# Shared-expert phase of a macaron network: logits two units behind a tile's turn, choice and places one unit later

## The reference, cut to what matters

```
h_s = _experts_mlp(u, g_shared, W1_s, b1_s, W2_s, b2_s).sum(axis=-2)
scores = jax.nn.sigmoid(u @ centroids)
gpk, i_topk = jax.lax.top_k(scores, K)            # K = 2 of 8
gk = gpk / scores.sum(axis=-1, keepdims=True)
routed_all = _experts_mlp(u, g_routed, W1_r, b1_r, W2_r, b2_r)
routed_topk = jnp.take_along_axis(routed_all, i_topk[..., None], axis=2)
h_r = (gk[..., None] * routed_topk).sum(axis=-2)
return u + h_s + h_r
```

## Time and profile before

| What | Value |
|---|---|
| median of 3 runs | 2846.81 us (2840.81 to 2848.97) |
| the profiled execution | 2843.61 us, span 2841.7 us |
| busy: PE, DVE, ACT, POOL | 82%, 70%, 50%, 44% of the span |
| ffn1a, shared-expert phase | about 1230 to 1494 us of the span |
| ffn1b, shared-expert phase | about 2216 to 2478 us of the span |
| granted TensorE clock, mean over the span | 0.904 of full |

### The profile page before, as it was taken

How to read it: one execution, slowest core, us unless ns; L and a number is a source line. 1 busy time by engine, 2 the same in 40 slices (tenths; PEclk the granted TensorE clock), 3 DMA queues, 4 the chain that set the end, 5 groups by cost and what they waited for, 6 DMA issues and landing times. The chain is left out here.

```text
span 2841.7 us, 51583 instructions
## 1 busy us (share of the span) xinstructions
PE 2337.6 (82%) x14828; PEld 1665.2 (59%) x14828; DVE 1996.4 (70%) x5346; ACT 1414.1 (50%) x2782; POOL 1258.1 (44%) x1094
## 2 busy tenths in 40 slices
PE   6559898999999896778898899388888788898890
PEld 5435454454444454756776677266667676677670
DVE  7666666666676665778786677388887787776675
ACT  4204454455454444656665566333332767566560
POOL 3242311221131122628773555476665287745551
PEclk9759999999999997888999999699999888999995
DMA  2031122121122213411135566110000111356556
GB/s 65 15 42 28 26 35 36 25 34 32 31 29 32 36 24 83 156 49 37 43 111 171 202 218 218 52 30 22 22 15 0 37 41 41 126 180 214 201 197 178
DMA packets 140628, 222.67 MB, mean 78 GB/s; under 512 B 21327, under 2 KB 100993, under 8 KB 129884
## 3 DMA queue, kind: packets, MB, share of 16 engines
q1 hardware_dynamic: 122203, 185.46, 23.8%
q0 software_dynamic: 18176, 34.14, 3.5%
HBM read 136.75 MB, written 57.32 MB: 68 GB/s over the span
## 5 line engine op out<-in xcount | busy, mean ns | idle before, releaser
L951 DVE TENSOR_REDUCE attn_rowmax<-psum 128x1 f32<-128x512 f32 (+3 forms) x748 | 457.3, 637 | 290.5 <-PE psum L789 289.8
L733 ACT ACTIVATE attn_probs<-psum 128x512 f32<-128x512 f32 (+1 forms) x704 | 387.0, 560 | 486.5 <-PE psum L852 478.7
L787 PE MATMUL psum<-attn_ks,attn_qs 72*128 72x512 bf16 (+3 forms) x1088 | 311.2, 321 | 39.4 <-DVE attn_rowmax L951 32.4
L850 PE MATMUL psum<-attn_qs,attn_ks 75*128 75x512 bf16 (+3 forms) x1024 | 288.0, 313 | 36.7 <-issue 26.2
L1287 POOL DMA_INDIRECT experts_answers<-ffn1b_y_rows,ffn1b_out_row x156 | 155.9, 999 | 151.9 <-ACT ffn1b_y_rows L1357 111.9
L789 PE MATMUL psum<-attn_mask_qk,attn_ident_b 128*128 128x128 bf16 x1088 | 222.0, 229 | 0.0
L1287 POOL DMA_INDIRECT experts_answers<-ffn1a_y_rows,ffn1a_out_row x156 | 156.9, 1006 | 146.8 <-ACT ffn1a_y_rows L1357 108.9
L850 PEld LDWEIGHTS psum<-attn_qs,attn_ks 75*128 75x128 bf16 x1024 | 101.0, 100 | 190.1 <-ACT attn_probs L733 99.5
L649 POOL TENSOR_TENSOR attn_rstd<-attn_var_eps,minus_half 128x4 f32<-128x4 f32 x18 | 18.3, 1019 | 436.4 <-DVE attn_var_eps L928 436.4
L852 PE MATMUL psum<-attn_mask_kq,attn_ident_b 128*128 128x128 bf16 x1024 | 204.0, 225 | 0.0
L867 PE MATMUL psum<-attn_probs,attn_v_aug 128*32 128x512 f32 (+3 forms) x2048 | 196.7, 462 | 0.0
(11 more groups left out here) (424 smaller groups left out, 6430.9 us busy)
## 6 DMA issues: line engine op xcount, KB each, us to landing
ffn1a_w_ring<-experts_packed SPq DMA_DIRECT2D x39, 1026.5 KB, 5.1
ffn1b_w_ring<-experts_packed SPq DMA_DIRECT2D x39, 1026.5 KB, 5.2
attn_qs<-attn_qparts SPq DMA_DIRECT2D x216, 64.0 KB
attn_ks<-attn_kparts SPq DMA_DIRECT2D x216, 64.0 KB
ffn1a_x_in<-experts_slots SPq DMA_DIRECT2D x39, 264.0 KB, 4.8
ffn1b_x_in<-experts_slots SPq DMA_DIRECT2D x39, 264.0 KB, 4.8
gla_answers<-experts_answers SPq DMA_DIRECT2D x32, 256.0 KB, 3.1
ffn1b_h<-experts_answers SPq DMA_DIRECT2D x16, 512.0 KB, 5.5
```

What stands on the lines that cost most here:

```text
L733: act.activation(probs[:, j % RING, 0:n], ps_exp[j % 2][:, 0:n], ACT.Exp, scale=SCALE).then_inc(exp_ready, 1)
L787: pe.matmul(out, qs[k][0:K_QK, 4 * g + hh, qt * P:(qt + 1) * P], ks[k][0:K_QK, 4 * g + hh, 0:n_keys], start=True, stop=False)
L850: pe.matmul(out, ks[k][:, 4 * g + hh, kt * P:(kt + 1) * P], qs[k][:, 4 * g + hh, kt * P:N], start=True, stop=False)
L951: dve.tensor_reduce(rowmax[:, NT - 1 - w, h:h + len(heads)], score_bank(n, j)[:, 0:len(heads) * width_of(w)].rearrange("p (a c) -> p a c", ...
```

## The change

Four tables of units are shifted by one. For tile r the logits go from one unit behind its turn to two. For a group, the exponent goes from two units behind the odd tile's turn to three, the choice of experts from three to four, rank, places and scatter from five to six. `totals_at` is worked out from `rank_at` and follows, from unit 27 to 28. The turns, moments, preparations and normalisations stay where they are.

```
     turn_at = {r: (3 * (r - 1) + 1) // 2 if r else -1 for r in range(S)}
     tile_turned = {u: r for r, u in turn_at.items()}
-    logits_at = {turn_at[r] + 1: r for r in range(S)}
-    exp_at = {turn_at[2 * g + 1] + 2: g for g in range(GROUPS)}
-    best_at = {turn_at[2 * g + 1] + 3: g for g in range(GROUPS)}
-    rank_at = {turn_at[2 * g + 1] + 5: g for g in range(GROUPS)}
+    logits_at = {turn_at[r] + 2: r for r in range(S)}
+    exp_at = {turn_at[2 * g + 1] + 3: g for g in range(GROUPS)}
+    best_at = {turn_at[2 * g + 1] + 4: g for g in range(GROUPS)}
+    rank_at = {turn_at[2 * g + 1] + 6: g for g in range(GROUPS)}
     moments_at = {r - 3: r for r in range(3, S)}
     prepare_at = {turn_at[r] - 2: r for r in range(2, S)}
     normalise_at = {turn_at[r] - 1: r for r in range(2, S)}
     totals_at = max(rank_at) + 1
```

## The result

The changed kernel takes 2933.53 us (median of 4 runs, 2928.69 to 2939.29), the kernel before on the same chip 2847.89 us. The ratio is 1.031, 95% interval 1.029 to 1.033: 3% slower, as forecast (2939, 2905 to 2970). A second timing beside the experiments gave 1.032 (1.030 to 1.034).

What follows compares the result with a forecast made beforehand. GpSimd's scatter stream was taken to bound both shared-expert stages. Per stage 6.6 + 45 - 5.5 = 46 us, twice 92, on the profiled 2843.6 gives 2936, as median 2939 us; range 2905 to 2970.

Steps and rivals of the forecast that it cites:

- The bound: Both shared-expert stages: GpSimd's stream of indirect scatter DMAs sets the end of the phase and the pace inside.
- Whole-scatter coupling: Groups 1 to 5: next scatter's places must wait for the whole previous scatter, odd half included; 45 us added per stage.
- One of its signs: GpSimd's idle ahead of scatters 1 to 5, put down to DVE's rows, would be 60 us in place of 8.
- First scatter: Start of each stage: the first places move one unit on DVE, so the scatter starts 6.6 us later.
- What comes back: Scatters of groups 0 to 4: fewer DVE casts beside them shorten the DMAs, 5.5 us back per stage.
- Logits later: PE's wait at L1414 for DVE's previous logits stays about as it is; if it went, nothing would follow.
- Rival B: PE's clock falls in long idle, too slow to feed gelu between scatter halves; 2990 us, chance 0.08.
- C: Rival: scatters of groups 0 to 4 shrink to bare DMAs, 15.5 us busy, 22 us more back; 2917 us, chance 0.04.
- D: Rival: only a shift, the odd half not ending last, each stage moving 5 us; 2857 us, chance 0.05.
- E: Rival: faster, PE's waits at L1414 were the bound and go; 2816 us, chance 0.03.

Runs made afterwards that it cites:

- e4: Changed kernel, all late tables kept, with eight slots of the xs ring in place of six; ratio 0.999 (0.996 to 1.001) to the kernel before.
- e8: Changed kernel, all late tables kept, with seven slots of the xs ring in place of six; ratio 0.998 (0.996 to 1.000) to the kernel before.
- e7: Changed kernel with choice, rank, places and scatter one unit later still; 2999.8 us in one run.
- e3: Changed kernel with odd tiles' normalise, from tile 7, behind gelu in the turn's unit, and rank and places issued first; ratio 1.021 to the kernel before.
- e5: Kernel before with eight slots of the xs ring in place of six; ratio 0.996 (0.994 to 0.998).
- e2: Changed kernel with rank, places and scatter alone back at five units behind the odd tile's turn; ratio 1.011 to the kernel before.
- e2b: As e2, but rank and places go ahead of the logits where they meet in one unit; ratio 1.019 to the kernel before.
- e6b: Kernel before with rank, places and scatter one unit earlier, ahead of the logits where both fall in one unit; ratio 1.013.

## Why the prediction was right, step by step

- *The bound* was read rightly: GpSimd's stream. Between the first memset and the stream's end the stages took 43.9 and 44.9 us more, 88.8 together, against 92 in the sum. The rest of the span was 3.7 us shorter, in both directions in its parts (4.4 more ahead of ffn1a, 3.0 and 5.0 less behind each stage), which no step claims.
- *Whole-scatter coupling*: shown, by e4 and e8 (dependence gone, loss gone), e7 (paid once for each coupled group) and e3 (the wait for the odd half moved behind gelu, part gone, the rest a wait for the even half). The five gaps were 14.3, 15.0, 11.4, 12.3, 11.4 us in ffn1a and 14.5, 15.0, 11.7, 12.7, 11.4 in ffn1b; the sum had 14.4, 15.2, 11.7, 12.5, 11.7. One of its signs was misnamed: it looked for 60 us put down to DVE's rows, and the trace has 35.1; ahead of groups 1 and 2 the same wait stands at the inverse (9.12 and 9.86 us).
- *First scatter*: 7.3 and 6.4 us later for the forecast 6.6.
- *What comes back*: all eight scatters together were 7.5 us shorter in ffn1a and 6.3 in ffn1b, for 5.5. The five groups that the prediction named gave 4.8 and 3.6 us of it; the rest came mostly from the last one, 1.8 us, which has six casts beside it in place of eight and which the sum had left out. So that the term came near is in part luck. More casts beside go with longer DMAs. The Trainium skill, "SBUF — State Buffer", gives a reason in "SBUF: two separate sides", that GpSimd can't write descriptors while DVE holds the shared ports, and the direction agrees, though no run here tests the reason; the 3100 ns of its section "A bandwidth-pool intuition that's wrong" are not seen: the longest DMA of the scatter is 1.72 us in both kernels.
- *Logits later*: "stays about as it is" was wrong. PE's wait at L1414 fell from 17.4 to 6.0 us in ffn1a and from 13.4 to 7.7 in ffn1b. That goes with the slower tiles, not with the later logits: in e8, with the same late logits and the tiles back at their old pace, it is 22.1 us in ffn1a. It had no price either way, as said.
- *Rival B*, PE too slow, did not come in the changed kernel, where gelu followed ACT's step before it at once; but in e3, where gelu no longer waits for the odd half, PE was what it waited for (3.67 us). *C* is out: scatters 0 to 4 were busy 17.9 us each on average in ffn1a, not the 15.5 of bare DMAs. *D* and *E* are out: the loss was 86 us where a shift would have cost 10, and PE's waits at L1414 shrank without a gain.

The price of the place itself, six or five units behind the turn, free of coupling and of the bank, can be read between e4 and e5 at eight slots: 0.999 and 0.996, intervals that overlap a little (5.3 us between the medians), with the streams ending 5.4 us apart in ffn1a and 3.9 in ffn1b. Rival D had put that shift at 5 us a stage; in the changed kernel it is hidden under the coupling.

## What to carry to other kernels

When an order written out by hand is moved, list for each moved step which blocking waits stand ahead of it in program order on every engine that it depends on, at the old place and at the new. Here one place further put the producer of a DMA stream behind the wait for the same stream's end, so two things that had overlapped took turns, and the price came in every group. One more ring slot (2.1 kB of each partition) bought that back; two made the order of before 0.4% faster than it was.

## What was not expected

Rank and logits in one unit cost more than expected in each of three kernels (e2, e2b, e6b), because both go through PSUM bank 5: PE waits 4.6 to 5.6 us on average, seven times a stage, until DVE has emptied it, with its down product queued behind. And PE's granted clock was lower where it stalled more: beside the scatters of groups 0 to 4 of ffn1a it was 0.80 to 0.93 before and 0.62 to 0.78 in the changed kernel, beside that of group 6, where nothing is coupled, 1.00 in both; over the span 0.904, 0.89 and, in e7, 0.879.
